# A transformer kernel's second attention: turned score steps 0 to 3 beside the first scores 5 to 13

## What is computed

```python
scores = jnp.einsum('bhtd,bhsd->bhts', q, k_enh) * SCALE
scores = jnp.where((diffs >= 0)[None, None], scores, -jnp.inf)
attn = jax.nn.softmax(scores, axis=-1)
out = jnp.einsum('bhts,bhsd->bhtd', attn, v_enh)
```

## Time and profile before

| | |
|---|---|
| three timed runs | 1112.11, 1114.26, 1116.97 us, median 1114.26 |
| profiled execution | 1112.5 us, its span 1110.8 us |
| PE busy | 965.3 us (87%) |
| DVE busy | 762.4 us (69%) |
| ACT busy | 592.5 us (53%) |
| POOL busy | 336.2 us (30%) |
| mean granted clock of PE | 0.923 |
| attention B, first score to last product | 731.2 to some 1017 us |

### The profile page before, as it was taken

How to read it: one execution, slowest core, us unless ns; L and a number is a source line. 1 busy time by engine, 2 the same in 40 slices (tenths; PEclk the granted TensorE clock), 3 DMA queues, 4 the chain that set the end, 5 groups by cost and what they waited for, 6 DMA issues and landing times. The chain is left out here.

```text
span 1110.8 us, 18644 instructions
## 1 busy us (share of the span) xinstructions
PE 965.3 (87%) x6218; PEld 624.7 (56%) x6218; DVE 762.4 (69%) x2256; ACT 592.5 (53%) x1165; POOL 336.2 (30%) x422
## 2 busy tenths in 40 slices
PE   6889999999999999999739376889999999997474
PEld 4666667666767676777528333344444444443464
DVE  6767758676677676666613699787888888862423
ACT  4866657666766666567312291314556565564121
POOL 2522122211221211122234107453644344521423
PEclk9999999999999999999759698868999999999577
DMA  6540000000000000000440100000000000000623
GB/s 202 120 115 2 1 1 1 1 1 1 1 1 1 1 1 1 1 1 1 126 124 31 46 1 0 1 1 1 1 1 1 1 2 1 1 1 1 202 61 100
DMA packets 49402, 32.23 MB, mean 29 GB/s; under 512 B 9195, under 2 KB 45980, under 8 KB 49308
## 3 DMA queue, kind: packets, MB, share of 16 engines
q1 hardware_dynamic: 47260, 26.78, 8.5%
q0 software_dynamic: 2048, 4.26, 1.2%
HBM read 21.44 MB, written 11.69 MB: 30 GB/s over the span
## 5 line engine op out<-in xcount | busy, mean ns | idle before, releaser
L562 ACT ACTIVATE attn_a_prob<-attn_a_score,attn_a_m_all 128x128 f32<-128x128 f32 (+7 forms) x256 | 188.7, 740 | 50.9 <-DVE attn_a_m_all L482 47.0
L912 ACT ACTIVATE attn_b_probT<-attn_b_st 128x1024 f32<-128x1024 f32 (+1 forms) x192 | 145.2, 808 | 131.7 <-PE attn_b_st L778 130.4
L478 DVE TENSOR_REDUCE attn_a_m_far<-attn_a_score 128x1 f32<-128x512 f32 (+3 forms) x192 | 105.6, 550 | 78.6 <-PE attn_a_score L390 76.4
L402 PE MATMUL attn_a_slot<-tab,attn_a_prob 128*128 128x128 f32 x1152 | 148.8, 273 | 1.4 <-ACT attn_a_prob L562 1.2
L402 PEld LDWEIGHTS attn_a_slot<-tab,attn_a_prob 128*128 128x128 f32 x1152 | 131.7, 140 | 9.8 <-issue 2.1
L414 PE MATMUL attn_a_o<-attn_a_ptsb,Vd 128*64 128x512 f32 x288 | 136.4, 603 | 0.0
L414 PE MATMUL attn_a_o<-attn_a_ptsa,Vd 128*64 128x512 f32 x288 | 136.4, 603 | 0.0
L841 DVE CUSTOM_DVE_ANT_0 attn_b_slot<-attn_b_slot,later 128x128 f32<-128x128 f32 (+3 forms) x256 | 118.5, 520 | 18.8 <-PE attn_b_slot L753 18.7
L571 ACT ACTIVATE attn_a_ptsa<-attn_a_slot 128x512 f32<-128x512 f32 x144 | 85.8, 596 | 80.7 <-PE attn_a_slot L402 80.0
L753 PE MATMUL attn_b_slot<-KS,attn_b_alone 128*128 128x512 f32 (+2 forms) x384 | 125.4, 424 | 2.8 <-POOL attn_b_alone L934 2.3
L482 DVE CUSTOM_DVE_ANT_0 attn_a_score<-attn_a_score,bias_near,attn_a_m_far 128x256 f32<-128x256 f32 (+2 forms) x192 | 107.4, 559 | 6.8
(11 more groups left out here) (236 smaller groups left out, 1828.4 us busy)
## 6 DMA issues: line engine op xcount, KB each, us to landing
moe_weights_w<-in_L_ffn_w_dram SPq DMA_DIRECT2D x32, 256.0 KB, 3.3
to_experts<-xn SPq DMA_DIRECT2D x2, 1056.0 KB, 11.9
moe_experts_xe<-to_experts SPq DMA_DIRECT2D x16, 132.0 KB, 2.6
bias_by_query_and_key<-bias_by_distance SPq DMA_DIRECT2D x2, 1024.0 KB
bias_near<-bias_by_query_and_key SPq DMA_DIRECT2D x2, 1024.0 KB, 6.2
from_experts<-xn SPq DMA_DIRECT2D x2, 1024.0 KB, 11.8
moe_experts_back<-from_experts SPq DMA_DIRECT2D x8, 256.0 KB, 3.8
X<-in_L_attn_a_x_dram SPq DMA_DIRECT2D x2, 512.0 KB, 4.6
```

The source lines that it names most:

```text
L402: ins = nc.tensor.transpose(dst[:, jj * P:(jj + 1) * P], probs(g)[:, 2 * jj + half, i * P:(i + 1) * P], ident[:, :])
L478: nc.vector.tensor_reduce(least, score[t % 2][:, at:at + nk - win], AX.X, ALU.min).then_inc(far_done, 1)
L562: nc.scalar.activation(probs(g)[:, j, 0:nk], score[t % 2][:, at:at + nk], ACT.Exp, bias=m_all[:, j:j + 1], scale=-1.0, accum_out=rowsum[g ...
L912: nc.scalar.activation(probT[n % 2][:, two, lo:], st[:, two, lo:], ACT.Exp, scale=-1.0).then_inc(exp_done, 1)
```

## The change

The order is now a table, `SCHEDULE`, of pairs: the turned step n (or none), and the first-score steps issued with it. Five steps of first scores stand alone (LEAD). With n = 0 come steps 5, 6, 7; with n = 1, 8 and 9; with n = 2, 10 and 11; with n = 3, 12 and 13. From n = 4 on the lag is 10 as before. Within an entry PE issues the turned step, the first two scores of its first-score steps (four if the first step is small), the product of the step before, then the other scores, then the turn of the shift values of the entry before. In the changed file PE's lines of this function have numbers 2 higher (L753 is L755), DVE's 1 lower (L871 is L870), POOL's 2 lower.

```diff
@@ -640,7 +640,10 @@
     PER = len(S_STEPS)
     GROUPS = BATCH * NG
     STEPS = GROUPS * PER
-    LAG = 10
+    LAG, LEAD = 10, 5
+    FIRST = ((5, 6, 7), (8, 9), (10, 11), (12, 13))
+    SCHEDULE = [(None, (m,)) for m in range(LEAD)] + [(n, FIRST[n] if n < len(FIRST) else (n + LAG,) if n + LAG < STEPS else ())
+                                                      for n in range(STEPS + 3)]
     VW = V9.shape[-1]
     RING, SLOTS_S = 4, 3
 
@@ -668,15 +671,14 @@
         diag_before.append(diag_before[-1] + on_diagonal(n))
     chunk_ends = [n for n in range(STEPS) if ends_chunk(n)]
 
-    def turns_max(n):
-
-        m = n + LAG - 1
-        return m if 0 <= m < STEPS and half_of(m) is not None else None
+    def turns_max(e):
+
+        halves = [m for m in SCHEDULE[e - 1][1] if half_of(m) is not None] if e else []
+        return halves[0] if halves else None
 
     def turns_out(n):
 
-        k = n - 2
-        return k if 0 <= k < STEPS and ends_chunk(k) else None
+        return n - 2 if n is not None and 0 <= n - 2 < STEPS and ends_chunk(n - 2) else None
 
     def s_part(m):
 
@@ -688,12 +690,12 @@
         return s_part(m)[2] <= BANK // 2
 
     slot, opened = {}, 0
-    for n in range(-LAG, STEPS + 3):
-        if n + LAG < STEPS:
+    for e, (n, ahead) in enumerate(SCHEDULE):
+        for m in ahead:
             for a in range(GRP):
-                slot["s", n + LAG, a] = opened
-                opened += a % 2 or not is_small(n + LAG)
-        for kind, k in (("max", turns_max(n)), ("out", turns_out(n))):
+                slot["s", m, a] = opened
+                opened += a % 2 or not is_small(m)
+        for kind, k in (("max", turns_max(e)), ("out", turns_out(n))):
             if k is not None:
                 slot[kind, k] = opened
                 opened += 1
@@ -801,25 +803,22 @@
                     ins = nc.tensor.transpose(dst[:, j * P:(j + 1) * P], blocks[:, j, :], ident[:, :])
                 ins.then_inc(slot_filled, 1)
 
-            for n in range(-LAG, STEPS + 3):
-                m = n + LAG
-                now, ahead = 0 <= n < STEPS, m < STEPS
-                if now:
+            for e, (n, ahead) in enumerate(SCHEDULE):
+                if n is not None and n < STEPS:
                     scores_t(n, 0)
                     scores_t(n, 1)
                     shifts_t(n, 0)
                     shifts_t(n, 1)
-                together = GRP if ahead and is_small(m) else GRP // 2
-                if ahead:
-                    for a in range(together):
-                        scores(m, a)
-                if 0 <= n - 1 < STEPS:
+                issued = [(m, a) for m in ahead for a in range(GRP)]
+                together = GRP if ahead and is_small(ahead[0]) else GRP // 2
+                for m, a in issued[:together]:
+                    scores(m, a)
+                if n is not None and 0 <= n - 1 < STEPS:
                     values(n - 1)
-                if ahead:
-                    for a in range(together, GRP):
-                        scores(m, a)
-                if turns_max(n) is not None:
-                    k = turns_max(n)
+                for m, a in issued[together:]:
+                    scores(m, a)
+                if turns_max(e) is not None:
+                    k = turns_max(e)
                     pe.wait_ge(max_ready, halves_before[k] + 1)
                     turn(slot["max", k], cols[k // PER % 2][:, half_of(k) * HALF:(half_of(k) + 1) * HALF, :])
                 if turns_out(n) is not None:
@@ -888,15 +887,14 @@
                 nc.vector.tensor_tensor(dst, got[:, :, :, 0:B_DH], r[:, :, :].unsqueeze(3).to_broadcast([P, HALF, GRP, B_DH]),
                                         ALU.mult).then_inc(slot_free, 1)
 
-            for n in range(-LAG, STEPS + 3):
-                m = n + LAG
-                if m < STEPS:
+            for e, (n, ahead) in enumerate(SCHEDULE):
+                for m in ahead:
                     for a in range(GRP):
                         row_least(m, a)
                     if half_of(m) is not None:
                         finish_max(m)
-                if turns_max(n) is not None:
-                    place_shift(turns_max(n))
+                if turns_max(e) is not None:
+                    place_shift(turns_max(e))
                 if turns_out(n) is not None:
                     normalize(turns_out(n))
 
@@ -935,14 +933,14 @@
                                         hmask.unsqueeze(2).to_broadcast([P, GRP, P]), ALU.mult).then_inc(q_alone, 1)
 
             made = 0
-            for n in range(-LAG, STEPS):
-                need = tile_of(min(n + LAG + 1, STEPS - 1)) + 3
+            for n, ahead in SCHEDULE:
+                need = tile_of(min(ahead[-1] + 1, STEPS - 1)) + 3 if ahead else GROUPS * QT
                 while made < min(need, GROUPS * QT):
                     query_alone(made)
                     made += 1
                 if n in (0, PER):
                     bias_out(n // PER)
-                if n >= 0 and on_diagonal(n):
+                if n is not None and n < STEPS and on_diagonal(n):
                     c, kt, lo = t_part(n)
                     for pair in range(2):
                         pool.wait_ge(exp_done, 2 * n + pair + 1)
```

## The result

| | before | changed |
|---|---|---|
| median of 17 runs | 1114.26 us (1111.73 to 1116.97) | 1118.31 us (1115.10 to 1122.47) |
| ratio | | 1.0039, 95% interval 1.0027 to 1.0051 |
| profiled execution, its span | 1112.5, 1110.8 us | 1120.38, 1118.6 us |
| first score of attention B | 731.17 | 733.06 |
| T4's shifts, counted from there | 33.42 | 35.20 |

The medians are 1118.31 - 1114.26 = 4.05 us apart (0.36%); the ratio on record puts the cost at 0.39%. It falls short of the half per cent that the prediction set as its bound, and the time lies above the range. Where it went: 1.8 us up to T4, 2.4 us behind it, both in attention B.

A forecast was written before the change was run, and what follows sets the result against it. DVE, then PE at 1.2 GHz, bound the stretch before turned step 4. DVE's 18.76 us of work plus waits of 1.6, 0.45, 1.8 and 0.19 made that step 1.2 us later: 1113.4 + 1.2 = 1114.6 us, range 1110.0 to 1117.5.

The forecast's parts named there:

- the half per cent: Whole kernel: no difference under 0.5% (5.6 us) is told from no change; no change had chance 0.91.
- the one number to forecast: Start of turned step 4's shift matmuls, 764.59 us before; a microsecond there is one of the kernel.
- the clock rises and falls again: Rival: PE's clock drops back to 0.50 before turned step 4; +5.2 us, 1118.6 us, chance 0.05.
- The chain up to T4: Waits and DVE work until turned step 4's shifts: 22.9 us behind the first shift copy, 21.7 before.
- The waits: DVE idles 1.6 us before first-score step 5, 0.45 before step 8, 1.8 before step 8's third reduction.
- ACT's idle time: ACT's idle before its first exp falls from 23.10 to about 14.5 us.
- POOL's bias copy: POOL's 2.37 us copy precedes turned step 0's masks, done 0.8 us before its value product's turn; costs nothing.
- The clock's rise: PE at 0.50 until turned step 0's value product, 9.5 us behind the first shift copy, then 1.0.
- PE's price of 0.575 us for a first score: Each 512-column first score at the lower clock takes 0.575 us; 0.43 would make the sum +0.9, not +1.2.
- The floor as the whole prize: DVE's work to the second shift copy with least waiting: at most 2.5 us gained, 0.22% of the kernel.
- the late clock: Rival: PE's clock stays low through the value product of turned step 1; +3.2 us, 1116.6 us, chance 0.17.
- the base of 1113.4: Median of four executions of the kernel before, to which the forecast added 1.2 us.

The follow-up runs named there:

- e1: Changed kernel with PE's two waits ahead of turned step 4 filled by 28 matmuls repeating that step's scores; 1114.42 us, ratio 1.0012.
- e10: Changed kernel with POOL's two query tiles of n=3 held back until DVE's join of maxima is finished; 1111.71 us, ratio 1.0018.
- e6: Changed kernel with 24 added matmuls into the idle pv bank around its five lone first-score steps; 1116.09 us, ratio 1.0020.
- e4: Kernel before with 44 added matmuls into the idle pv bank, ahead of and behind its lone first scores; 1111.52 us, ratio 0.9979.
- e2: Changed kernel with first-score step 13 moved from turned step 3's entry to step 4's, so the second shift copy comes earlier; 1115.49 us, ratio 1.0019.
- e3: Changed kernel with the second of POOL's two query tiles at n=3 asked for one step later; 1119.67 us, ratio 1.0047.
- e7: Changed kernel with both of POOL's query tiles of n=3 made one step later, without holding POOL back; 1117.52 us, ratio 1.0035.
- e12: Kernel before with 44 added matmuls into the idle pv bank, an unchanged repeat of e4; 1111.63 us, ratio 0.9988.
- e8: Kernel before with only the second shift turn and its copy moved behind first-score step 13; 1118.23 us, ratio 1.0035.
- e9: Unchanged repeat of e8, the kernel before with only the late second shift copy; 1110.27 us, ratio 1.0008.

## Why the prediction was wrong

- **The step that failed: that everything behind T4 stays as it was.** The prediction made T4's start "the one number to forecast" and a microsecond of T4 a microsecond of the kernel. So its sum holds nothing for PE's clock behind T4, and the case in which it falls became a rival, "the clock rises and falls again", with a chance of 0.05. That is what happened: 0.53 from 767.80 to 774.60, and 253.57 us behind T4 instead of 251.19. With the waits filled (e1) it was 251.31. The prediction wrote down that PE has some 5 us of work in 8 from S11 to T4 (measured 5.37 in 8.08), and then weighed it by the absence of a row that shows a fall. But the earlier trace rows from 764.60 have PE busy 99% and say nothing of a stretch where it waits, and the trace of before has a fall at 998.00, right behind their end.
- **Its price:** 4 us for the fall, from 4 us of work at half the clock, where 2.4 were measured. The clock was down for 6.8 us, and at half the clock PE does in them what takes 3.4 at the full one, so more than 3.4 us could not be lost (an estimate from these rows). That the rival's total of 1118.6 lies so near 1118.31 is luck: its fall was too dear, its way up to T4 too cheap (1.2 for 1.8 us), and it stood on 1113.4, where 17 runs of the kernel before have 1114.26.
- **The chain up to T4: right in its steps, 0.6 us short in its sum.** Forecast 22.9 us behind the first shift copy, measured 23.45, before 21.7. The waits: 1.6, 0.45 and 1.8 forecast, 1.62, 0.41 and 1.64 measured. T1 5.1 us behind the copy, measured 5.25; ACT's idle time 14.5, measured 14.02. POOL's bias copy stayed off the path, as said: T0's masks ended at 751.05, PV0 started at 752.15.
- **The clock's rise: right in this profile, in part by luck.** Forecast with PV0, 9.5 us behind the copy; measured 9.4. In e1, with the same work up to there, it rose 5.8 us behind the copy, ahead of PV0, and T4 came 21.89 us behind the copy. The prediction treated the rise as fixed by PE's work. PE's price of 0.575 us for a first score of 512 columns at 0.50, which it kept over an estimate of 0.43, was met: S8's first two took 752.15 - 751.00 = 1.15 us.
- **A term left out:** POOL's tiles beside DVE's join. The prediction looked at POOL's queue for what waits on it, not for what runs beside it. 0.9 us more in the join (1.67 against 0.77), which e10 takes away again (0.75). It also lengthened PE's wait ahead of S13 (1.45 us, 0.43 in e10), though the clock fell in e10 too. Part of it doesn't show in the sum: from the end of the first copy to the end of the second DVE worked 19.57 us, not 18.76, but waited 3.82 instead of 4.04.
- **The floor as the whole prize** (2.5 us, T4 19.2 us behind the first copy) was not reached: with the changed order at the full clock, e6, it is 20.77. The old order at the full clock, e4, has 19.04, as its second copy doesn't stand behind S13.
- **The range** was built from the DVE floor to the late clock and left the falling clock out. With that case in, it would have reached 1118.6 and held 1118.31. Of the 3.7 us between the forecast of 1114.6 and 1118.31, 0.9 are the base of 1113.4 from four executions, 0.6 the chain up to T4, and most of the rest the fall.
- **The weighed rule.** The Trainium skill, "TensorE: Matmul & The Clock Gate", section "A second HAM failure mode: psum-queue depth-cycling", says that short idles between groups that cycle through PSUM banks make the clock swing between its levels. The trace agrees in kind, with a single swing: up at 754.20, down at 767.80, up at 774.60, behind waits of 1.45 and 0.91 us. It does not agree everywhere: e2 has such waits (1.11 and 0.46 us) and no fall. By that rule the time would have been the rival's 1118.6.

## What to carry to other kernels

Moving PE work from a stretch where PE is full into one where another engine sets the pace also thins PE out there. Before such a move, add up PE's work in each piece of the new order at the full clock; where PE is left waiting in several pieces, count the lower clock behind it as a likely case, whatever long steady rows show, and read the clock over the whole trace, also where the rows that you picked end. And list for the moved work not only who waits for whom, but which POOL operations will run beside the small SBUF operations of DVE.

## What the runs showed of the hardware

- A DVE operation of 16 columns on SBUF operands that starts just behind a two-operand POOL operation of 1.04 us did not end before it: L855 took 1.02 in the changed kernel instead of 0.17 to 0.33, L862 0.98 in e3, L860 and L862 0.99 and 0.97 in e7, 0.18 and 0.20 in e10 with no tile beside them. DVE's reductions from PSUM beside the same tiles kept their 0.65 us pitch (in the changed kernel they start at 761.90, 762.54 and 763.19 with a tile at 762.03). The Trainium skill, "SBUF — State Buffer", section "🔬 SBUF: two separate sides", states the rule: VectorE and GpSimd share a pair of SBUF ports under an exclusive lock, and whichever starts first keeps it for the whole instruction; VectorE needs the pair when its operation has two SBUF inputs, or runs in a mode that uses two ports. The trace agrees for an operation with two SBUF inputs (L855, 1.02 us). L860 in e7 has a single SBUF input and was held too (0.99 us); whether it ran in such a mode the profile doesn't show.
- Matmuls that compute nothing new paid for themselves twice: 28 in e1 for the clock behind them (ratio 1.0012 against the changed kernel's 1.0039), 44 in e4 and e12 for the clock from the start (0.9979 and 0.9988). The kernel that does more work is the faster one.
- The granted clock of a stretch can differ between executions of equal instructions. The dips near 30 us of the first attention do: the next stage starts at 545.23 in e8 and 542.40 in e9, the same kernel. The late fall of attention B does too: 1.3 us inside the stage in e8, none in e9. What sets them was not tried.
